# Four-tile accumulation in the edge stage of a graph network: 8-node one-hot places set into a bank of 20 nodes

## The reference, cut to what matters

```python
_s = jax.random.randint(jax.random.fold_in(_gk, 2), (50000,), 0, 3125, jnp.int32)
_d = jax.random.randint(jax.random.fold_in(_gk, 3), (50000,), 0, 3125, jnp.int32)
src = jnp.concatenate([_s, _d, _loop])
dst = jnp.concatenate([_d, _s, _loop])
_o = jnp.argsort(dst, stable=True)
...
# layer 0: one graph convolution; layer 1: three, with edge weights; layer 2: two, with graph norm
agg = jax.ops.segment_sum(h[src] * norm[:, None], dst, num_segments=n)
# layer 3: attention per edge, 8 heads of 12
score = jnp.exp(jnp.clip((K[src] * Q[dst] * E / sqrt(12)).sum(-1), -5.0, 5.0))
out = segment_sum(V[src] * score, dst) / (segment_sum(score, dst) + 1e-06)
```

## Time and profile before

| what | value |
|---|---|
| median of 3 runs | 2583.65 us (2583.22 to 2584.04) |
| the profiled execution's own time | 2575.93 us |
| its span in the profile | 2574.1 us |
| busy: PE, DVE, ACT, POOL | 2014.7, 1459.5, 1053.4, 921.1 us |
| `examine_edges` | 0 to about 30 us |
| `add_edges` | about 30 to 684 us |
| `graph_layers` | about 684 to 1490 us |
| `attention_windowed`, then the output | about 1490 to 2538 us, to 2574 us |

### The profile page before, as it was taken

The page is one execution under the profiler, slowest core; times in us unless marked ns, Lnnn a source line. Parts: engine busy times, 40 slices in busy tenths (PEclk is TensorE's granted clock), DMA queues, the critical chain, the costliest instruction groups (busy, mean ns, idle before and its releaser), DMA issues. The chain is left out here.

```text
span 2574.1 us, 48365 instructions
## 1 busy us (share of the span) xinstructions
PE 2014.7 (78%) x14338; PEld 1700.0 (66%) x14338; DVE 1459.5 (57%) x3333; ACT 1053.4 (41%) x2976; POOL 921.1 (36%) x884
## 2 busy tenths in 40 slices
PE   2888788788599999999989557777777777777772
PEld 1555455455378999999868346676767667667672
DVE  8999899899643111144232445555555555555555
ACT  5899889898522000011121323333333333333330
POOL 0022122212000000000000267777777777777771
PEclk9999999899789999999989555555555555555555
DMA  1456656465768877777646175555555555555541
GB/s 51 61 100 106 95 94 109 80 110 93 136 211 301 289 289 286 295 279 274 211 162 218 42 181 160 156 161 158 157 161 161 161 155 160 159 159 158 161 130 37
DMA packets 226425, 416.22 MB, mean 162 GB/s; under 512 B 131915, under 2 KB 151393, under 8 KB 216545
## 3 DMA queue, kind: packets, MB, share of 16 engines
q1 hardware_dynamic: 187485, 334.92, 46.8%
q0 software_dynamic: 38784, 79.48, 11.7%
HBM read 347.87 MB, written 66.43 MB: 161 GB/s over the span
## 5 line engine op out<-in xcount | busy, mean ns | idle before, releaser
L2225 POOL DMA_INDIRECT attention_windowed_vkv<-kv_dram,ttention_windowed_vsrc x808 | 777.4, 962 | 247.0 <-issue 225.6
L2308 PE MATMUL attention_windowed_vps_s<-attention_windowed_hot,attention_windowed_vmsg 128*104 128x32 f32 x1616 | 322.0, 363 | 270.1 <-DVE attention_windowed_vmsg L2365 268.4
L646 ACT ACTIVATE add_edges_hot_lo<-add_edges_hot_lo,add_edges_parts 128x128 bf16<-128x128 bf16 x1616 | 488.2, 387 | 66.9 <-DVE add_edges_hot_lo L754 66.4
L2308 PEld LDWEIGHTS attention_windowed_vps_s<-attention_windowed_hot,attention_windowed_vmsg 128*104 128x104 f32 x1616 | 295.1, 288 | 311.2 <-DVE attention_windowed_vmsg L2365 250.7
L684 PE MATMUL add_edges_ps_pair<-add_edges_hot,add_edges_hot_lo 128*128 128x300 bf16 x2424 | 450.0, 296 | 0.0
L2296 PE MATMUL attention_windowed_vps_e<-attention_windowed_vwe,attention_windowed_vattr 97*128 97x96 f32 x1616 | 404.2, 432 | 24.6 <-ACT attention_windowed_hot_T L2253 24.6
L1219 PE MATMUL graph_layers_acc<-graph_layers_w_tab,graph_layers_g 125*96 125x125 f32 x3750 | 417.7, 269 | 0.0
L1219 PEld LDWEIGHTS graph_layers_acc<-graph_layers_w_tab,graph_layers_g 125*96 125x96 f32 x3750 | 406.6, 163 | 0.0
L2296 PEld LDWEIGHTS attention_windowed_vps_e<-attention_windowed_vwe,attention_windowed_vattr 97*128 97x128 f32 x1616 | 368.8, 333 | 25.5 <-issue 25.4
L678 PE MATMUL add_edges_ps_pair<-add_edges_hot,add_edges_hot_lo 128*128 128x300 bf16 x808 | 241.6, 299 | 129.1 <-DVE add_edges_strip L785 84.5
L785 DVE TENSOR_TENSOR add_edges_strip<-add_edges_strip,add_edges_ps_pair 128x600 f32 x404 | 311.4, 771 | 17.3 <-PE add_edges_ps_pair L684 13.6
(11 more groups left out here) (233 smaller groups left out, 2159.3 us busy)
## 6 DMA issues: line engine op xcount, KB each, us to landing
graph_layers_w_tab<-w_blocks SPq DMA_DIRECT2D x75, 1562.5 KB
graph_layers_c_tab<-c_blocks SPq DMA_DIRECT2D x75, 800.0 KB
w_blocks<-add_edges_strip SPq DMA_DIRECT2D x25, 1562.5 KB, 16.4
attention_windowed_vattr<-in_attr_T SPq DMA_DIRECT2D x202, 192.0 KB
attention_windowed_vdrow<-dstf_dram SPq DMA_DIRECT2D x202, 192.0 KB
c_blocks<-add_edges_counts SPq DMA_DIRECT2D x25, 800.0 KB, 14.5
attention_windowed_vkv<-kv_dram,ttention_windowed_vsrc POOLq DMA_INDIRECT x808
ttention_windowed_q_rows<-q_dram SPq DMA_DIRECT2D x202, 18.0 KB
```

Of the source, the lines that this page charges most:

```text
L646: done = nc.scalar.activation(hot_lo[s][:, 1 + part, j, :], hot_lo[s][:, 0, j, :], ACT.Copy, scale=parts[:, part, bass.ds(g * G + j, 1)])
L2225: nc.gpsimd.indirect_dma_start(out=kv[s][:, k, :], out_offset=None, in_=kv_dram, in_offset=bass.IndirectOffsetOnAxis(ap=src4[s][:, k:k + 1 ...
L2308: last = nc.tensor.matmul(ps_s[s % 2][:], msg[s][:, k, :], hot[s][:, k, :], start=k == 0, stop=k == Q4 - 1)
```

## The change

The constants change from `WINDOW` = 12 to `WINDOW` = 8 and `REACH` = 20. A tile's one-hot of places now has 25 x 8 = 200 columns, counted from the tile's own first node. TensorE sums four tiles instead of two in one buffer of two banks, 25 x 20 = 500 columns each (`ps_four`): it clears the bank with two matmuls of zeros, and writes each tile's 25 x 8 columns at an offset that it loads into a register (`in_reach`, the tile's first node less the quad's first node). DVE adds 1000 columns per quad instead of 600 per pair, and takes over half of the second weight parts from ACT (`middle`, 4 of 8 tiles). The order of DVE's loop is written out for all rounds instead of a loop. The check computes the new conditions: row 2 of `slack` now asks that a tile's nodes lie within 8 of its first, and row 3 that a tile's first node lies within `REACH - WINDOW` = 12 of the quad's first; the earlier row 3, the quad within 32 nodes, follows from these two. The branch is taken on the same flag as before.

```diff
-WINDOW = 12
+WINDOW = 8
+REACH = 20
...
-        strip = mem.sb("strip", [P, 2, NT, RING + WINDOW])
+        strip = mem.sb("strip", [P, 2, NT, RING + REACH])
...
-        ps_pair = [mem.ps(f"ps_pair{s}", [P, 2, BANK]) for s in range(2)]
+        ps_four = [mem.ps(f"ps_four{s}", [P, 2, BANK]) for s in range(2)]
...
-                        for part in range(2):
+                        for part in range(2 if j < BY_ACT else 1):
...
+            def spots(g):
...
+                _, at = nc.values_load_multi_w_load_instructions(in_reach[0:1, bass.ds(G * g, G)], engines=(mybir.EngineType.PE,), min_val=0,
+                                                                 max_val=REACH - WINDOW, skip_runtime_bounds_check_because=why)
+                return at
...
-                    for j in range(4):
-                        p = 4 * g + j
...
-                            nc.tensor.matmul(out[:, 0, 0:PLACES], hot_lo[s][:, 0, e, :], hot[s][:, e, :], start=m == 0, stop=m == 1)
+                    at = spots(g)
+                    for u in range(2):
+                        q = 2 * g + u
+                        pe.wait_ge(hot_ready, q + 1)
+                        if reaches(q, 2):
+                            pe.wait_ge(added, q - 1)
+                        both = ps_four[u]
+                        for table in range(2):
+                            nc.tensor.matmul(both[:, table, 0:NT * REACH], nought[:], noughts[:], start=True, stop=False)
+                        for m in range(Q4):
+                            e = Q4 * u + m
...
+                            cells = both[:, :, 0:NT * REACH].rearrange("p c (t n) -> p c t n", n=REACH)[:, :, :, bass.ds(at[e], WINDOW)]
+                            nc.tensor.matmul(cells[:, 0], hot_lo[s][:, 0, e, :], hot[s][:, e, :], start=False, stop=m == Q4 - 1)
...
+            def middle(g, s):
+                n, m = P // 2, G - BY_ACT
+                table = middle2[:, bass.ds(g * G + BY_ACT, m), :].unsqueeze(2).broadcast_to((P, m, n, 2))
+                nc.vector.tensor_tensor(pairs(hot_lo[s][:, 2, BY_ACT:G, :], n), pairs(hot_lo[s][:, 0, BY_ACT:G, :], n), table, ALU.mult)
...
-            rounds(dve, body)
+            rounds(dve, body, written_out=True)
...
-            nc.vector.tensor_tensor(slack[:, 2, :].rearrange("p (q k) -> p q k", k=2),
-                                    first[:].rearrange("p (q k) -> p q k", k=2)[:, :, 0].unsqueeze(2).broadcast_to((P, NPAIR, 2)),
-                                    dst_f[:].rearrange("p (q k) -> p q k", k=2), ALU.subtract)
+            nc.vector.tensor_tensor(slack[:, 3, :].rearrange("p (q k) -> p q k", k=Q4), first[:].rearrange("p (q k) -> p q k", k=Q4),
+                                    steps.unsqueeze(2).broadcast_to((P, NQ, Q4)), ALU.subtract)
...
-            nc.vector.tensor_scalar(slack[:, 3, :], rel[:], -1.0, SPAN_Q - 1.0, ALU.mult, ALU.add)
+            nc.vector.tensor_copy(in_reach[:], slack[0:1, 3, :])
+            nc.vector.tensor_copy(dst_f[:], slack[:, 0, :])
+            nc.vector.tensor_scalar(slack[:, 2, :], slack[:, 0, :], -1.0, WINDOW - 1.0, ALU.mult, ALU.add)
...
-            nc.vector.tensor_scalar(slack[:, 2, :], slack[:, 2, :], WINDOW - 1.0, None, ALU.add)
+            dve.drain()
+            nc.vector.tensor_scalar(slack[:, 3, :], slack[:, 3, :], -1.0, float(REACH - WINDOW), ALU.mult, ALU.add)
```

131 lines of the change are left out of this document (66 added, 65 removed).

## The result

The changed kernel takes 8904.83 us (median of 4 runs, 8903.85 to 8908.37), the kernel before 2583.43 (4 runs, 2582.62 to 2584.04); the ratio is 3.447, with a 95% interval from 3.441 to 3.453. The prediction was 8550 us, and the reason it gave is the one that the trace shows: the first branch isn't taken. The profiled execution has a span of 8902.6 us.

What follows compares the result with a forecast made beforehand. DVE was taken to bound `add_edges`, TensorE `graph_layers`, POOL `attention_windowed`. With the general path taken instead, 32 + 277 + 1545 + 574 + 125 + 895 + 5070 + 40 = 8558 us, forecast 8550, range 6850 to 10300.

Steps and rivals of the forecast that it cites:

- terms 2 and 4: Zeros in `build_adjacency`, 80.3 MB, 277 us; `first_pass`, 160.6 MB, 554 us plus about 20; both at 290 GB/s.
- term 3: Scatters in `build_adjacency`: 101 batches of eight at 1.6 us plus a landing of 2.5, 15.3 us each, 1545 us.
- term 7: `attention_general`: 202 steps of 25.1 us, each a closed chain of waits, 5070 us.
- 5 two small phases: `first_layer_out` at 75 us and `attention_tables` at 50 us.
- term 6: `convolutions`: 700 us of products at 2.4 GHz, 35 us between passes, 20 to start; 895 us.
- The ring: In `attention_general`, landing, `prepare`, `attend`, products, copy and POOL's issues wait on each other in turn, 25.1 us a step.
- the second rival: In `attention_general` the ring is not closed; POOL alone sets a step, 16.5 us, total 6820 us; chance 0.12.
- The third: Accumulating scatters cost two gathers, 2.52 us, and land late, in `build_adjacency` and `attention_general`: 10.27 ms; chance 0.16.
- The fourth: In `build_adjacency` DVE's comparisons hold up POOL, 5.6 us more a batch, total 9120 us; chance 0.2.
- The kept branch: If the flag were 1, the edited `add_edges` would run, 73 us less, 2511 us; chance 0.02.
- the rival: With the first branch kept, up to 2570 us if DVE waits for TensorE in `add_edges`; within that case's chance of 0.02.

Runs made afterwards that it cites:

- experiment 2: Changed kernel with the check's limit 13 instead of 12, TensorE's offset held to 12 and a spacer added: 2571.25 us, 0.997 times the kernel before.
- Experiment 1: Kernel before, with its check narrowed to 16 nodes instead of 32 so that it takes the general path: 8910.28 us, 3.452 times the kernel before.
- 3: Changed kernel with `WINDOW` = 6 instead of 8 and a spacer added: 2648.41 us, 1.028 times the kernel before.
- experiment 7: Changed kernel with offset held to 12, such tiles' places counted from there, TensorE's clearing before its wait, and a spacer: 2565.42 us, 0.995 times the kernel before.
- experiment 11: Changed kernel with both its indirect scatters writing their rows instead of adding them: 7834.69 us.
- experiment 5: Changed kernel with `attend` put ahead of `prepare` on VectorE in `attention_general`: 8494.79 us.
- Experiment 6: Changed kernel with the eight comparisons of `build_adjacency` written as `tensor_tensor` instead of `tensor_scalar`: 8988.14 us.

## Why the prediction was right

**The check.** As predicted, the flag falls and the edited code doesn't run. That 18 of 202 quads are over the limit is worked out from the inputs; that the furthest is one over it, experiment 2 shows. Experiment 1 separates this from everything else in the edit, and experiments 2, 3 and 7 show the other side: with the limit met, the time is 2565 to 2650 us.

**The sum.** 8558 was worked out and 8904.8 measured, 4% more, inside the range and inside the sum's own range of 7600 to 9600. That it came so near is partly luck, since errors of both signs stand behind it: terms 2 and 4 were 251 us too dear, terms 3 and 7 together 690 too cheap.

| term | predicted, us | trace, us | where the size was off |
|---|---|---|---|
| 1 start and check | 32 | 35 | |
| 2 zeros | 277 | 204 | 80.3 MB in 204 us, 394 GB/s where 290 was taken |
| 3 scatters | 1545 | 1790 | 17.6 us a batch, not 15.3 |
| 4 `first_pass` | 574 | 396 | 409 GB/s at a DMA share of 0.96 |
| 5 two small phases | 125 | 108 | |
| 6 `convolutions` | 895 | 823 | |
| 7 `attention_general` | 5070 | 5515 | 27.3 us a step, not 25.1 |
| 8 output | 40 | 32 | |

In terms 2 and 4 I took a rate of 290 GB/s, from a stage in which the DMA engines were busy for 0.81 of the time, and gave as the reason that these are writes; the trace bears out no such discount. With the 369 GB/s at full share, which the same row gives, they would have been 673 us and not 851, against 600 measured. The rule of the Trainium skill's page "DMA: Bandwidth & Descriptors" (section "Anatomy of one DMA — SWDGE (gpsimd) path") was weighed there. An estimate from its 436 GB/s is 184 + 388 = 572 us for the two, and the trace's 600 lies nearer to it than to my 851. Its 2.0 us fixed are near the landing of 1.9 us in term 7; in term 3 the landing is 2.4, nearer to my 2.5. For terms 2 and 4 the page was the better guide; the whole sum by it, 8.13 ms, lies further from the 8.90 measured than mine.

Term 3 was too cheap. An adding scatter takes 1.54 us and 0.30 to the next, 1.84 and not 1.6: in the earlier trace rows the gather is 0.96 + 0.30, and I put the price of the addition at 0.34 where experiment 11 shows 0.57. Up to four of eight are up to 0.23 longer beside comparisons, so the mean of all 808 is 1.64. 8 x 1.64 + 7 x 0.30 + 2.4 = 17.6; the landing of 2.4 us was right. In term 6 the granted clock read 0.93, near the level of 2.4 GHz that the term assumed, so the 700 us that the range kept for the lower one were not needed.

Term 7: the issues are 15.4 us in place of 14.0 (again the adding scatters, 1.91 apart and not 1.6, and gathers 1.34 apart and not 1.26), `prepare` 3.3 in place of 3.0, products and copy 2.9 in place of 2.6, and 0.9 us pass between ScalarE's copy and GpSimd's first scatter, of which the sum had nothing. Landing (1.9 for 2.5) and `attend` (2.9 for 3.0) were a little cheaper. In all 1.4 + 0.3 + 0.3 + 0.9 - 0.6 - 0.1 = 2.2 us a step. What was mis-sized is above all the adding scatter's price, and what was missing is the hand-over.

**The rivals.** The ring is closed (experiment 5), so the second rival is out. The third, two gathers' time for a scatter, is out by size: 1.84 of the 2.52 us. The fourth, GpSimd held up by VectorE's comparisons, exists at 0.8 us a batch and not 5.6, 78 us in all (808 x (1.639 - 1.542)). The Trainium skill's page "SBUF — State Buffer" (section "Who interferes with whom") has VectorE's fast forms block GpSimd for a whole instruction, and an instruction of two tensors in SBUF contend with GpSimd's reads. Both forms did lengthen the scatters here, by 0.23 and by 0.43 us, but neither held GpSimd up for as long as it ran itself (0.770 and 1.217 us a comparison, more than one beside most scatters), so a block of that size is not what this kernel shows. Experiment 6 doesn't tell which of the two rules is at work, and what the engines contend for was not found. A plain scatter loses only 0.08 beside comparisons (1.05 against 0.97), which suggests, but doesn't show, that it hangs on the work of adding.

**The kept branch.** 2511 us was worked out and 2571 measured, at the edge of the rival's "up to 2570" (by the ratio, 0.997 of 2583 is 2576). Its reason, VectorE waiting for TensorE, is the one that the trace shows. The step of this side sum that failed was costing "at nothing" TensorE's clearing of the banks, as "behind DVE there": it stood between the places and the add, 0.66 us a quad. With it moved ahead, the traced execution of experiment 7 has half of the wait left, while the medians moved by only 6 us. What the other half waits for was not taken apart.

## What to carry to other kernels

Before reading what a new fast branch costs, work out from the inputs' distribution whether its guard holds: a limit of 12 stood beside a mean of 11.6, and 18 of 202 cases past it cost 6300 us, where the edit, made to hold and mended, gave 14. In a stage in which no engine is busy all the time, follow one turn of the ring in the timeline and price each hand-over; from VectorE's or ScalarE's last instruction to GpSimd's next it was 0.9 us in this ring, each turn. It is no fixed price: ahead of the first scatter of `build_adjacency` it was 0.2 us (VectorE's end at 239.43 us, GpSimd's start at 239.65), and what fills the longer ones the trace doesn't show. Work that an idle engine does is free only if it doesn't stand between a wait and the result that the bound engine wants.

## What the runs showed of the hardware

An indirect DMA that adds took GpSimd 1.54 us beside 0.97 for one that writes, for the same 128 rows, and 112 packets more. Beside VectorE's comparisons it took 1.77 or 1.97 us by their form. Products of 150 columns in place of 200 came with a granted clock of 0.53 to 0.66 in place of 0.88 to 0.97 and were the slower ones, 0.33 against 0.27 us; in another kernel they took 0.33 us with a granted clock that read 1.00. Filling DRAM with zeros went at 394 GB/s at a DMA share of 0.99, where the kernel before loaded its tables at 299 at a share of 0.81.
